# A gated cross-attention block with routed experts on one core: splitting early weights in parts, another order of the first units, and one packed flag word for the output scatters

## What is computed

```python
xn = layer_norm(_layernorm(x), ln_g, ln_b)
cn = layer_norm(ctx_1024, cln_g, cln_b)
q = (xn @ Wq) per head * 64 ** -0.5;  k, v = split(cn @ Wkv)
out = softmax(q @ k.T) @ v @ Wo
h, gate = split(xn @ Wff1)
out = out + silu(gate) * h @ Wff2
x = x + tanh(g_xattn) * out
xf = _layernorm(x)
shared = silu(xf @ sh_up_w + sh_up_b) @ sh_down_w + sh_down_b
topk_w, topk_i = top_k(softmax(xf @ gate_w.T), 2)      # normalised
y[n] = sum over the two experts e of w * (silu(xf @ up_w[e] + up_b[e]) @ down_w[e] + down_b[e])
return x + tanh(g_ffn) * (y + shared)
```

## Time and profile before

| | us |
|---|---|
| median of 3 runs (534.63 to 535.72) | 534.79 |
| profiled execution, its own time | 536.77 |
| its span | 534.6 |
| PE busy | 496.8 (93%) |
| DVE, ACT, POOL busy | 406.7, 327.2, 288.4 |
| first and last start of the 39 output scatters | 446.0, 525.0 |

### The profile page before, as it was taken

One profiled execution on the slowest core, in us unless ns is written; L12 is line 12 of the kernel. 1 busy time (PEld: TensorE's weight loads), 2 busy tenths in 40 slices (PEclk: granted clock), 3 DMA queues, 4 the chain that ended last, 5 costly groups with the idle time before them and its releaser, 6 DMA issues.

```text
span 534.6 us, 13846 instructions
## 1 busy us (share of the span) xinstructions
PE 496.8 (93%) x4026; PEld 482.5 (90%) x4026; DVE 406.7 (76%) x1253; ACT 327.2 (61%) x1092; POOL 288.4 (54%) x332
## 2 busy tenths in 40 slices
PE   7779999999999999999999999999999989999940
PEld 7669999999999999999999999999998779999930
DVE  6677778788787878786888888787677888888830
ACT  2576657675665675657566756675567727767730
POOL 2488627553643554364445436553685334677773
PEclk9899999999999999999999999999999999999995
DMA  5552300102003010301210030004398976788753
GB/s 170 196 155 85 99 2 33 31 25 105 31 20 118 21 29 11 118 32 30 78 61 21 20 118 31 10 28 141 118 345 298 408 267 141 132 136 145 114 65 39
DMA packets 40213, 53.85 MB, mean 101 GB/s; under 512 B 4598, under 2 KB 34219, under 8 KB 39147
## 3 DMA queue, kind: packets, MB, share of 16 engines
q1 hardware_dynamic: 31856, 41.48, 23.6%
q0 software_dynamic: 8000, 11.86, 11.9%
q10 hardware_dynamic: 314, 0.01, 0.0%
HBM read 28.15 MB, written 25.21 MB: 100 GB/s over the span
## 4 chain that ended last, share of the span: by engine, by line
PE 60%; DVE 11%; issue 8%; DMA 7%; POOLq 5%; ACT 5%; POOL 3%; SPq 0%; DVEq 0%; ACTq 0%
PE bank L1544 12%; PE bank L1546 11%; PE bank L1545 11%; DMA out_x<-norm_probs,th 5%; PE bank L1625 5%; POOLq L729 4%; PE bank L1637 4%; PE bank L1730 4%; PE bank L1720 4%; PE bank L1641 3%; PE bank L1628 2%; PE bank L1735 2%; PE bank L1559 2%; DVE norm_probs L1012 2%; ACT norm_probs L818 2%
## 5 line engine op out<-in xcount | busy, mean ns | idle before, releaser
L628 POOL TENSOR_TENSOR norm_probs<-norm_probs,rden 128x512 f32<-128x512 f32 x64 | 66.5, 1040 | 101.2 <-DVE rden L1192 100.4
L1544 PE MATMUL bank<-acts,weights 128*128 128x256 f32 x384 | 110.1, 287 | 5.3 <-POOL weights L599 5.3
L1545 PE MATMUL bank<-acts,weights 128*128 128x256 f32 x384 | 108.6, 283 | 0.0
L1546 PE MATMUL bank<-acts,weights 128*128 128x256 f32 x384 | 108.3, 282 | 0.0
L818 ACT ACTIVATE norm_probs<-bank,nmax 128x128 f32<-128x128 f32 x256 | 90.4, 368 | 23.8 <-DVE nmax L1148 23.8
L633 POOL TENSOR_TENSOR acts<-uf,acts 128x256 fp32r<-128x256 f32 x64 | 47.5, 742 | 68.7 <-ACT acts L806 68.7
L1544 PEld LDWEIGHTS bank<-acts,weights 128*128 128x128 f32 x384 | 73.3, 191 | 6.2 <-issue 5.0
L742 POOL DMA_INDIRECT out_x<-norm_probs,th x39 | 60.7, 1557 | 25.6 <-DMA out_x<-norm_probs,th 14.2
L1546 PEld LDWEIGHTS bank<-acts,weights 128*128 128x128 f32 x384 | 73.1, 190 | 0.0
L1545 PEld LDWEIGHTS bank<-acts,weights 128*128 128x128 f32 x384 | 73.0, 190 | 0.0
L806 ACT ACTIVATE acts<-uf 128x256 fp32r<-128x256 f32 x64 | 26.8, 419 | 61.3 <-DVE uf L1217 61.2
(11 more groups left out here) (251 smaller groups left out, 1544.5 us busy)
## 6 DMA issues: line engine op xcount, KB each, us to landing
parked<-stage SPq DMA_DIRECT2D x12, 512.0 KB, 3.5
weights<-parked SPq DMA_DIRECT2D x6, 1024.0 KB
slot_rows<-tf SPq DMA_DIRECT2D x8, 680.0 KB, 6.6
spare<-slot_rows SPq DMA_DIRECT2D x39, 136.0 KB
ct<-in_ctx SPq DMA_DIRECT2D x8, 256.0 KB, 2.7
xs<-in_x SPq DMA_DIRECT2D x8, 256.0 KB, 4.8
stage<-in_L_ffn_up_w SPq DMA_DIRECT2D x8, 256.0 KB, 2.8
stage<-in_L_ffn_down_w SPq DMA_DIRECT2D x8, 256.0 KB, 3.1
```

What stands on the lines that cost most here:

```text
L628: pool.tensor_tensor(pr[:, s % 2], pr[:, s % 2], rden[:, s % 2, :].unsqueeze(2).broadcast_to((P, 4, P)), ALU.mult).then_inc(probs_ready, 1)
L1544: pe.matmul(ps, wts[1], mov[0], start=first, stop=False, skip_group_check=True)
L1545: pe.matmul(ps, wts[0], mov[0], start=False, stop=False, skip_group_check=True)
L1546: return pe.matmul(ps, wts[0], mov[1], start=False, stop=last, skip_group_check=True)
```

## The change

Two independent parts.

**The start.** Chunks 1, 2 and 4 are handed over in parts (`LO_PARTS`): PE's first two query products wait for the first half of the low parts of chunks 1 and 2 only, and each unit's product with chunk 4 for its quarter. Chunk 1's low part becomes two halves on DVE, the second at the end of the prologue. The high part of the key/value weights moves from DVE to ACT, its low part (`key_weights`) behind the second `transposed`; the split of the gate weights (`gate_parts`) moves from DVE's prologue into unit 3. Before the first group ACT splits chunks 4 and 6, not 4 and 5; DVE, not POOL, makes the low parts of 6 and 5 (units 0 and 1); POOL's slots go from chunks 6 to 10 in units 0 to 4 to chunks 7, 8, 10, 9 in units 2 to 5. In unit 0, `hidden_values` (`u1`, `uf`) comes right behind the maximum and ahead of the reciprocal; the statistics of the next group (2 steps) move from the end of unit 0 to behind the maximum of unit 1. SP loads chunk 6 ahead of the context and input of group 1, and chunk 5 behind them.

**The scatters.** DVE counts the tokens once more after the seventh group and computes flags for distances one, two and three; they are packed in one word (bits 4, 5, 6). POOL loads one word per tile, cuts it with shifts and masks, always waits for scatter t-4 and only where due for t-3.

```diff
-EARLY = 6
-CHUNK_SLOT = {0: [6], 1: [7], 2: [8], 3: [9], 4: [10]}
-LO_ON_POOL = (2, 4, 5, 6, 7, 8, 9, 10)
+CHUNK_SLOT = {2: 7, 3: 8, 4: 10, 5: 9}
+LO_ON_POOL = (2, 4, 7, 8, 10, 9)
+HI_ORDER = (1, 2, 3, 4, 6, 5, 7, 8, 10, 9)
+LO_PARTS = {1: 2, 2: 2, 4: 4}
...
                     done = pool.tensor_tensor(lo_i, src_i, hi_i.bitcast(F32), ALU.subtract)
-                done.then_inc(chunk_split_done[n], 1)
+                    if (i + 1) % (4 // LO_PARTS.get(n, 1)) == 0:
+                        done.then_inc(chunk_split_done[n], 1)
...
                 if t >= 1:
-                    due_1, due_2 = [pool.value_load(turns[t:t + 1, i:i + 1], min_val=0, max_val=16) for i in range(2)]
+                    due = pool.value_load(turns[t:t + 1, 0:1], min_val=0, max_val=112)
+                    due_1, due_2, due_3 = due & 16, (due >> 1) & 16, (due >> 2) & 16
+                if t >= 4:
+                    pool.wait_ge(y_added[t % 4], 16 * (t // 4) + 16)
                 if t >= 3:
-                    pool.wait_ge(y_added[(t - 3) % 4], 16 * ((t - 3) // 4) + 32)
+                    pool.wait_ge(y_added[(t - 3) % 4], due_3 + (16 * ((t - 3) // 4) + 16))
...
             split_hi(3)
+            landed(act, 0)
+            act.activation(wkv[0][:, :, :], stage[:, 0, 0:KT * P].rearrange("p (k n) -> p k n", k=KT), ACT.Copy
+                           ).then_inc(kv_hi_done, 1)
...
             transposed("TXx", None, False, False, 0)
-            early_lo(1)
+            early_lo(1, 0)
             first_lo(xnT, 1, xnT_ready)
             transposed("TXc", None, False, False, 0)
-            gate_cols = cols[:, :, 5:NROW]
...
+            key_weights()
+            first_lo(cnT, 2, cnT_ready)
...
             values_lo(None, False, False, 0)
+            early_lo(1, 1)
...
+                    if first and s == 0:
+                        hidden_values(s)
...
+                    if s == 1 and first:
+                        dve.wait_ge(ctx_loaded, 32)
+                        dve.wait_ge(x_in[1], 16)
+                        small_steps(2)
...
+                    if first and s < 2:
+                        early_lo((6, 5)[s])
+                    if first and s == 3:
+                        gate_parts()
...
+                for rows, at in ((slice(0, 3), slice(0, 3)), (slice(3, 5), slice(0, 2)), (slice(6, 7), slice(0, 1))):
+                    done = dve.scalar_tensor_tensor(due[:, rows, 0:NE - 1], margin[:, rows, 0:NE - 1], 0.0,
+                                                    opens[:, at, 0:NE - 1], ALU.is_gt, ALU.mult)
...
+                link(dve.scalar_tensor_tensor(turn_f[:, 0:1], turn_f[:, 1:2], 2.0, turn_f[:, 0:1], ALU.mult, ALU.add))
+                link(dve.scalar_tensor_tensor(turn_f[:, 0:1], turn_f[:, 2:3], 4.0, turn_f[:, 0:1], ALU.mult, ALU.add))
...
-            split(pe, 1)
-            split(pe, 2)
+            split(pe, 1, 1)
+            split(pe, 2, 1)
```

More of the change, by code:

```diff
@@ L683, in iteration @@
                         expert_lo(s - 4)
-                    if first:
-                        for n in CHUNK_SLOT.get(s, []):
-                            split_lo(n)
+                    if first and s in CHUNK_SLOT:
+                        split_lo(CHUNK_SLOT[s])
                 if not last:
@@ L796, in probs_hi, with hidden_high, hidden_tanh @@
                 act.activation(pT[0][:, :], t_ps[:, :], ACT.Copy).then_inc(pTh_done, 1)
+            def hidden_high(s, g, first, last):
+                u = g * NU + s
+                act.wait_ge(mix_freed, mix_index(f"FF{s}", g, first, last) + 1)
+                if not (first and s < 2):
+                    act.wait_ge(ff2_done, u - 1)
+                act.activation(uT[0][:, s % 2, :], uf[:, :], ACT.Copy).then_inc(uh_done, 1)
+            def hidden_tanh(s, g, first, last):
+                u = g * NU + s
+                b = mix_ps[mix_bank(f"FF{s}", g, first, last)]
+                act.wait_ge(mix_filled, mix_index(f"FF{s}", g, first, last) + 1)
+                if not (first and s == 0):
+                    act.wait_ge(u1_done, u)
+                act.activation(th[:, :], b[:, GT:2 * GT], ACT.Tanh, scale=0.5).then_inc(tanh_done, 1)
             def iteration(g, first=False, last=False):
@@ L800, in iteration @@
                     u = g * NU + s
[L801 to L806 removed]
+                    if 1 <= s <= NU and not (first and s == 1):
+                        hidden_high(s - 1, g, first, last)
+                    if first and s == 0:
+                        hidden_tanh(s, g, first, last)
                     if s == NU + 1 and last:
@@ L820, in iteration @@
                         done.then_inc(exp_done, 1)
-                    if first:
-                        for n in CHUNK_SLOT.get(s, []):
-                            split_hi(n)
+                    if first and s == 0:
+                        hidden_high(s, g, first, last)
                     if s == NU and not last:
@@ L1355, in window_shares @@
                     dve.memset(shares[:, k:k + 1], float(1 << (SHIFT * k)))
-                dve.tensor_scalar(late, hist[0], -1.0, float(P), ALU.mult, ALU.add)
-                dve.tensor_scalar(early, hist[1], -1.0, 2.0 * P, ALU.mult, ALU.add).then_inc(shares_done, 1)
+                for k in range(2):
+                    done = dve.tensor_scalar(missing[:, k, :], hist[k], -1.0, (k + 1.0) * P, ALU.mult, ALU.add)
+                done.then_inc(shares_done, 1)
                 dve.wait_ge(shares_done, 1)
@@ L1588, in queries @@
                 pe.wait_ge(xnT_ready, gn + 1)
+                if first and pair == 2:
+                    split(pe, 1)
+                    split(pe, 2)
                 for i in range(2):
@@ L1645, in iteration, with chunk @@
             def iteration(g, first=False, last=False):
-                def chunk(n):
+                def chunk(n, part=None):
                     if first:
-                        split(pe, n)
+                        split(pe, n, part)
                 def scores(s):
@@ L1722, in iteration @@
                     if 1 <= s <= NU:
[L1724 removed]
+                        chunk([4, 8][(s - 1) // 4], s if s < 5 else None)
                         if s == 1 and not first:
```

156 lines of the change are left out of this document (81 added, 75 removed).

## The result

| | before | changed |
|---|---|---|
| median, us | 535.25 | 529.86 |
| runs, us | 534.79, 535.72, 534.63, 536.68 | 527.8, 530.22, 530.09, 529.63 |
| ratio, 95% interval | | 0.9884 (0.9861 to 0.9907) |
| profiled execution, span | 536.77, 534.6 | 527.8, 526.1 |

The changed kernel is faster by 1.2%. The medians lie 5.4 us apart; the ratio, which is not the quotient of these two medians, stands for 6.2 us (5.0 to 7.4). The traced execution of the changed kernel is the fastest of its four, and that of before was slower than each of the four listed. So the two traces lie 9.0 us apart (536.77 - 527.8), more than the medians, and not everything in them may be put down to the change. The experiments come to that.

A forecast was written before the change was run, and what follows sets the result against it. PE was taken as the bound in the steady groups, so time was to be had only in the start and the scatters: 536.8 - 3.1 - 3.7 = 530.0, on the median 534.8 - 6.8 = 528.0 us; range 524.5 to 531.5.

The forecast's parts named there:

- Half hand-over and clock, -3.2 at the keys: Start: PE's queries begin 1.9 us earlier on half of chunk 2's low part; the kept 2.4 GHz clock saves 1.3 more.
- Waits of 3.6 us replaced by one of 2.3 for DVE: Units 1 and 2: PE's waits for probabilities and chunk 6 give way to one for DVE's low part, 29.9 to 32.2.
- The rival with DVE 2 us later: Start: DVE and POOL exclude each other, DVE bounds PE; start only -1.1, total -4.8, 530.0 us; chance 0.18.
- Chunk 9, +1.0: Start, unit 6: POOL splits chunk 9 until 62.4 while PE wants it at 61.44, a new PE wait of 1.0 us.
- The start in all, -3.1: Whole start: -4.1 us at 35 us plus 1.0 for chunk 9's wait; bounds 0 and -6.5.
- Scatters, 75.1 us for 38 steps: Tile loop: 38 steps at the 1.86 floor plus 2.6, 1.5 and 0.3 of waits, 75.1 us against 79.0.
- the stretch of slow loads of 1.5: Tile loop: loops of slower loads in POOL's queue were expected to stay, costing some 1.5 us.
- Flags at distance three, 0.8: Tile loop: scatter t-3 has 5.6 us to land; only one landing of 5.84 broke that, and its 0.8 us loss goes.
- DVE's delay at the tile loop, +0.2: Some three more small DVE operations ahead of the tile loop and four in tile 1 delay it by 0.2 us.
- The rival "slower", 543: Tile loop: dear register instructions lengthen each scatter step by 0.5 us, 18 us in all, kernel 543 us; chance 0.03.
- The step from the traced execution to the median, -2.0: Whole kernel: the profiled execution lies 2.0 us above the median, and the same difference was applied to the forecast of 530.0.

## Why the prediction was right, point by point

Forecast 528.0 us in a range of 524.5 to 531.5, measured 529.86; the fall of the medians was forecast as 6.8 us and was 5.4 (6.2 by the ratio). The mechanisms of both parts are borne out. That the total came within 2 us took some luck: terms that were off in one place met terms that were off in another.

- **Half hand-over and clock, -3.2 at the keys.** The first key product came 4.3 us earlier. 1.0 of it is the execution's, the earlier load of chunk 2 (POOL's split of it began at 12.52 instead of 13.52). That leaves 3.3. In the trace of the scatters alone, which has the start of before, the first key product is at 20.77, 3.4 later than in the changed kernel. The mechanism and the size are right. The argument for the clock was weak: that one idle stretch of 2.1 us kept it doesn't mean that the next does. The same stretch kept it in one trace of the changed kernel and lost it in another.
- **Waits of 3.6 us replaced by one of 2.3 for DVE.** The wait is from 29.49 to 31.63, 2.0 us beyond the usual pace; forecast 29.9 to 32.2. The transposes of unit 0 came at the time forecast but waited 1.08 us, where "hardly a wait" was said. The rival with DVE 2 us later fell short: the exclusion cost DVE 0.6 and POOL 0.9, not 2, and the small means took 0.17 us each and not 0.7. At 34 us PE is 4.7 us ahead, 3.7 without the earlier load; forecast 4.1. The forecast's own terms (3.6 of waits gone, 2.3, 0.6 and 0.4 come in) give 0.3 us beside the 3.2 and not the 0.9 that it added.
- **Chunk 9, +1.0.** PE's gap is 1.1 us, at the place forecast.
- **The start in all, -3.1.** As a mechanism right, as a mean too high: alone it is worth 1.9 us (0.9 to 3.0). The trace has PE 3.2 us ahead at 400 us, of which the earlier load is 1.0. Part of the rest can be the clock that some executions lose behind the stretch at 29.5 to 31.6, 1.5 us where it happens, and early loads of chunk 2, behind which the half hand-over saves nothing. How often either happens was not seen.
- **Scatters, 75.1 us for 38 steps.** 73.7 in the first trace: the floor of 1.86 held in 32 steps, the waits of scatters 6 and 8 cost 2.4 beyond it (forecast 2.6), four small ones 0.6, and the stretch of slow loads of 1.5 didn't come. But this trace is the shortest of the ten, and 75.1 is near the others (73.9 to 75.3) for another reason than the forecast's: in place of slow loads they have longer waits at 6 and 8 and waits at distance three, which the forecast had at nothing. The second load, put back, cost 0.5 us a step.
- **Flags at distance three, 0.8.** Too low a price in general: the step "distance three let scatter t-3 land in 5.6 us" failed, since a scatter begins 1.0 to 1.2 us behind the landing it waits for, so 4.4 to 4.6 us are left, and the run without the flags lost 2.2 us to two such waits in its trace.
- **DVE's delay at the tile loop, +0.2.** PE's lead over before shrank by 0.5 us there (3.3 to 2.8): the term was too small by 0.3. The trace of the start alone, which has the old table, keeps its lead at that place (3.6, then 3.7), which points at the larger table. The cause wasn't tried by itself.
- **The rival "slower", 543.** Its 18 us more and the start's 3.1 less give 550 and not 543. Its condition didn't come: in the changed kernel six register instructions fit under the floor of 1.86.
- **The step from the traced execution to the median, -2.0.** This is the mis-sized term. The sum for the traced execution was 530.0, and it took 527.8; but this one lies 2.1 below its median, while that of before lay 2.0 above. I carried the distance over as if it were the kernel's own. It is the execution's, and it has several causes: the load of chunk 2 (1.0 us between the two traces), the clock behind an idle stretch (1.5 us between the two traces of the changed kernel) and the landings of the scatters (1.6 us between these two).

## What to carry over

Give each wait of PE two prices: its length, and what the granted clock costs behind it in those executions in which it falls; an idle stretch of 2 us that kept the clock in one trace is no proof for the next. In a queue of small instructions between two long ones, first find the engine's own floor: an instruction under the floor is free, one above it counts in full in each round. And before the time of one trace is moved over to a median, take a second trace of the same kernel and see where the two part. The mean granted clock alone doesn't tell, since it counts the end of the kernel too, where PE has nothing left to do.

## What was not expected of the hardware

- The clock's fall is not settled by the idle stretch alone. In the start, 1.85 or 1.86 us of PE's idle time before the values' product kept 1.00 in five traces and were followed by 0.50 for 3.4 us in two; 2.20 us before the transposes kept it (before), 2.42 lost it (scatters alone). At the entry to the tile loop idle times of 1.31, 1.34 and 1.43 us kept it, and 1.32 and 0.97 lost it. The price in the start was 1.4 to 1.5 us where it was measured. What decides it wasn't found.
- Loads of a word into POOL's queue take 0.29 in one stretch and 0.6 to 0.7 in another; with two loads a turn every second turn was slow (steps of 2.24 and 2.56 us in alternation). This wasn't explained.
- Landings of a scatter, read from the last update of its semaphore, take 3.3 to 6.0 us, with medians of 3.8 to 4.5 in a trace. With the same scatter code the 38 steps took 73.7 to 75.3 us for them. No pattern in them was found.
